# One fp32 product per block in place of three fp16 products in an attention kernel

## What is computed

```
att = softmax(einsum('bmi,bmj->bij', k, q), axis=2)          # layer 0, per image
out = x + einsum('cm,bmn->bcn', wo, einsum('bij,bmj->bmi', att, v))
...
scores = where(causal, -1e30, einsum('bhqd,bhkd->bhqk', q, k) / D ** 0.5)   # layer 1
attn = softmax(scores, axis=-1)
out = einsum('bhqk,bhkd->bhqd', attn, v) ... @ Wo
```

## Time and profile before

| what | value |
|---|---|
| median of 3 runs | 653.6 us |
| the profiled execution's own time | 655.42 us |
| its span | 653.6 us |
| granted TensorE clock, mean share of full speed | 0.94 |
| busy: PE, DVE, ACT, POOL | 535.2, 497.6, 468.7, 442.0 us |

### The profile page before, as it was taken

How to read it: one execution, slowest core, us unless ns; L and a number is a source line. 1 busy time by engine, 2 the same in 40 slices (tenths; PEclk the granted TensorE clock), 3 DMA queues, 4 the chain that set the end, 5 groups by cost and what they waited for, 6 DMA issues and landing times.

```text
span 653.6 us, 17645 instructions
## 1 busy us (share of the span) xinstructions
PE 535.2 (82%) x6985; PEld 348.9 (53%) x6985; DVE 497.6 (76%) x1060; ACT 468.7 (72%) x891; POOL 442.0 (68%) x401
## 2 busy tenths in 40 slices
PE   3777769799779999878989977878999988984694
PEld 0234347466546666546666644555666655663241
DVE  4667877688888778888778888886777888845568
ACT  2167648998748888757888865567888867892673
POOL 2455647978848878757878874476888767893003
PEclk9978769999979999989999998799999989996798
DMA  8000000000000000000000000000000000000001
GB/s 225 33 2 2 1 1 3 2 2 2 3 2 2 2 3 2 2 1 3 2 2 3 2 2 2 3 1 1 2 3 2 2 2 3 3 3 2 0 0 64
DMA packets 2784, 6.46 MB, mean 10 GB/s; under 512 B 1008, under 2 KB 1296, under 8 KB 2576
## 3 DMA queue, kind: packets, MB, share of 16 engines
q1 hardware_dynamic: 2336, 4.30, 2.4%
q10 hardware_dynamic: 368, 1.05, 0.5%
HBM read 4.22 MB, written 1.05 MB: 8 GB/s over the span
## 4 chain that ended last, share of the span: by engine, by line
PE 48%; DVE 31%; ACT 8%; POOL 6%; issue 5%; DMA 1%; DVEq 0%; SPq 0%; ACTq 0%; POOLq 0%
PE bank L355 7%; DVE attn_partial_max L667 7%; POOL probs_low L637 5%; PE bank L381 5%; PE bank L382 5%; PE bank L318 4%; PE bank L408 4%; DVE queries_low L660 4%; PE bank L412 4%; PE bank L410 4%; ACT queries_high L540 4%; PE bank L319 3%; PE bank L514 3%; DVE probs_low L637 2%; DVE conv_partial_max L656 2%
## 5 line engine op out<-in xcount | busy, mean ns | idle before, releaser
L637 POOL TENSOR_TENSOR probs_low<-probs,probs_high 128x512 f16<-128x512 f32 x312 | 374.7, 1223 | 135.2 <-ACT probs_high L553 134.9
L552 ACT ACTIVATE probs<-bank 128x512 f32<-128x512 f32 x352 | 219.3, 623 | 26.3 <-PE bank L384 19.3
L553 ACT ACTIVATE probs_high<-bank 128x512 f16<-128x512 f32 x352 | 220.6, 627 | 0.0
L667 DVE TENSOR_REDUCE attn_partial_max<-bank 128x1 f32<-128x512 f32 (+2 forms) x288 | 195.1, 686 | 24.8 <-PE bank L355 16.9
L408 PE MATMUL bank<-values_high,probs_high 128*128 128x65 f16 x1408 | 169.8, 198 | 6.0 <-POOL probs_low L637 2.5
L410 PE MATMUL bank<-values_low,probs_high 128*128 128x64 f16 x1408 | 169.8, 196 | 0.0
L412 PE MATMUL bank<-values_high,probs_low 128*128 128x65 f16 x1408 | 169.5, 196 | 0.0
L408 PEld LDWEIGHTS bank<-values_high,probs_high 128*128 128x128 f16 x1408 | 135.8, 100 | 31.2 <-issue 7.3
L410 PEld LDWEIGHTS bank<-values_low,probs_high 128*128 128x128 f16 x1408 | 133.9, 101 | 21.6 <-issue 4.2
L355 PE MATMUL bank<-attn_keys,queries_high 128*128 128x512 f16 (+3 forms) x384 | 117.1, 332 | 34.2 <-DVE attn_partial_max L667 22.2
L412 PEld LDWEIGHTS bank<-values_high,probs_low 128*128 128x128 f16 x1408 | 134.0, 100 | 0.0
(11 more groups left out here) (152 smaller groups left out, 737.3 us busy)
## 6 DMA issues: line engine op xcount, KB each, us to landing
x_channels<-in_x_cm SPq DMA_DIRECT2D x7, 256.0 KB, 9.0
tokens<-in_x_tm SPq DMA_DIRECT2D x1, 1024.0 KB, 12.0
out<-ln_channels SPq DMA_DIRECT2D x4, 256.0 KB, 2.0
queries_high<-minus_max_rows SPq DMA_DIRECT2D x36, 2.0 KB
attn_weights<-in_attn_w ACTq DMA_DIRECT2D x1, 512.0 KB, 8.6
x_channels<-in_x_cm ACTq DMA_DIRECT2D x1, 256.0 KB, 3.7
constants<-in_const ACTq DMA_DIRECT2D x1, 256.0 KB, 5.9
conv_weights<-in_conv_w SPq DMA_DIRECT2D x1, 128.0 KB, 2.4
```

Source lines behind the costliest of these rows:

```text
L552: nc.scalar.activation(e32[:, i % E_RING, :], o[:], ACT.Exp, scale=scale)
L553: nc.scalar.activation(p_hi[:, i % P_RING, :], o[:], ACT.Exp, scale=scale).then_inc(s_probs, 1)
L637: eng.tensor_tensor(out=p_lo[:, i % P_RING, :], in0=e32[:, i % E_RING, :], in1=p_hi[:, i % P_RING, :], op=ALU.subtract).then_inc(done, 1)
L667: nc.vector.reduce_max(dst, src, AX).then_inc(s_prep_used, 1)
```

## The change

Probabilities stay in fp32 in one ring of ten buffers, written by one exponential per item. Values stay in fp32, written by one ACT copy. Each block takes one fp32 product in place of three of fp16. The subtractions for `probs_low` and `values_low` are gone from POOL and DVE, with their semaphores, and LAG goes from 5 to 3.

```diff
-ST_RING, MX_RING, P_RING, E_RING, Q_RING = 3, 2, 8, 6, 3
-LAG, REST_LAG = 5, 3
-CONV_DVE_RESTS, ATTN_DVE_RESTS = (5, 11), (4,)
+ST_RING, MX_RING, E_RING, Q_RING = 3, 2, 10, 3
+LAG = 3
...
             nc.tensor.wait_ge(s_probs, i + 1)
-            if rest_on_dve(i):
-                nc.tensor.wait_ge(s_rest_dve, dve_rests(i))
-            else:
-                nc.tensor.wait_ge(s_rest_pool, i + 1 - dve_rests(i))
-            hi, lo = p_hi[:, i % P_RING, :], p_lo[:, i % P_RING, :]
-            vh, vl = v_hi[v % 2], v_lo[v % 2]
+            probs, values = e32[:, i % E_RING, :], v32[v % 2]
...
-                    nc.tensor.matmul(dst, hi[:, cols], vh[:, j, :], start=opens, stop=False,
-                                     skip_group_check=True)
-                    nc.tensor.matmul(dst[:, 0:C], hi[:, cols], vl[:, j, :], start=False, stop=False,
-                                     skip_group_check=True)
-                    ins = nc.tensor.matmul(dst, lo[:, cols], vh[:, j, :], start=False, stop=True,
-                                           skip_group_check=True)
+                    ins = nc.tensor.matmul(OT[c][:, t * PO:t * PO + PO], probs[:, cols], values[:, j, :],
+                                           start=opens, stop=True, skip_group_check=True)
...
             if i >= E_RING:
-                if rest_on_dve(i - E_RING):
-                    nc.scalar.wait_ge(s_rest_dve, dve_rests(i - E_RING))
-                else:
-                    nc.scalar.wait_ge(s_rest_pool, i - E_RING + 1 - dve_rests(i - E_RING))
-            if i >= P_RING:
-                nc.scalar.wait_ge(s_values, i - P_RING + 1)
+                nc.scalar.wait_ge(s_values, i - E_RING + 1)
-            nc.scalar.activation(e32[:, i % E_RING, :], o[:], ACT.Exp, scale=scale)
-            nc.scalar.activation(p_hi[:, i % P_RING, :], o[:], ACT.Exp, scale=scale).then_inc(s_probs, 1)
+            nc.scalar.activation(e32[:, i % E_RING, :], o[:], ACT.Exp, scale=scale).then_inc(s_probs, 1)
...
-                nc.scalar.activation(v_hi[k % 2][:, :, 0:C], AUX[:].rearrange("p (t c) -> p t c", c=C),
-                                     ACT.Copy).then_inc(s_aux_cast, 1)
+                nc.scalar.activation(v32[k % 2][:, :, 0:C], AUX[:].rearrange("p (t c) -> p t c", c=C),
+                                     ACT.Copy).then_inc(s_aux_used, 1)
...
-        def rest_item(eng, i, done):
-            eng.wait_ge(s_probs, i + 1)
-            eng.tensor_tensor(out=p_lo[:, i % P_RING, :], in0=e32[:, i % E_RING, :], in1=p_hi[:, i % P_RING, :],
-                              op=ALU.subtract).then_inc(done, 1)
...
-            elif what == "values":
-                nc.vector.wait_ge(s_aux_cast, AUX_CASTS_BY[m])
-                nc.vector.tensor_tensor(out=v_lo[k % 2][:], in0=AUX[:].rearrange("p (t c) -> p t c", c=C),
-                                        in1=v_hi[k % 2][:, :, 0:C], op=ALU.subtract).then_inc(s_aux_used, 1)
```

More of the change, by code:

```diff
@@ L122, in auxes_at @@
     return [m for m, step in enumerate(AUXES) if step[0] == g]
[L125 to L132, removed]
 def build(nc, x_cm, x_tm, conv_w, conv_vo, attn_w, ffn, gb, const, out):
@@ L177, in build @@
         q_lo = [sb(f"queries_low{i}", [P, N], f16) for i in range(Q_RING)]
[L178 to L182, removed]
+        e32 = sb("probs", [P, E_RING, CW])
+        v32 = [sb(f"values{i}", [P, NT, PO]) for i in range(2)]
         scaled = sb("scaled_outputs", [P, NC, TPC, C])
@@ L257, in build @@
         s_probs = sem("probs_written")
-        s_rest_pool = sem("rest_by_pool")
-        s_rest_dve = sem("rest_by_dve")
         s_values = sem("values_accumulated")
@@ L406, in pe_values @@
                     cols = slice((at + k) * P, (at + k + 1) * P)
-                    dst = OT[c][:, t * PO:t * PO + PO]
-                    nc.tensor.matmul(dst, hi[:, cols], vh[:, j, :], start=opens, stop=False,
-                                     skip_group_check=True)
-                    nc.tensor.matmul(dst[:, 0:C], hi[:, cols], vl[:, j, :], start=False, stop=False,
-                                     skip_group_check=True)
-                    ins = nc.tensor.matmul(dst, lo[:, cols], vh[:, j, :], start=False, stop=True,
-                                           skip_group_check=True)
+                    ins = nc.tensor.matmul(OT[c][:, t * PO:t * PO + PO], probs[:, cols], values[:, j, :],
+                                           start=opens, stop=True, skip_group_check=True)
             ins.then_inc(s_values, 1)
@@ L824, in _ @@
                 nc.vector.memset(amx[i][:], -3e38)
-                nc.vector.memset(v_hi[i][:, :, C:PO], 1.0)
+                nc.vector.memset(v32[i][:, :, C:PO], 1.0)
                 nc.vector.memset(y16[i][:, :, 0:1], 0.0)
@@ L835, in _ @@
                         dve_rowmax(v)
-                if 0 <= g - REST_LAG < ITEMS and rest_on_dve(g - REST_LAG):
-                    rest_item(nc.vector, g - REST_LAG, s_rest_dve)
                 for m in auxes_at(g):
@@ L965, in _ @@
             for g in range(0, LAST_SLOT):
-                if g < ITEMS and not rest_on_dve(g):
-                    rest_item(nc.gpsimd, g, s_rest_pool)
                 for v, c in HALVES_AT.get(g, ()):
@@ L1014 @@
 CASTS_BY = [sum(k < (4 if v < B else 2) for _, v, k in PREPS[:m + 1]) for m in range(len(PREPS))]
-AUX_CASTS_BY = [sum(what in ("conv_matrix", "values", "matrix") for _, _, what, _ in AUXES[:m + 1])
+AUX_CASTS_BY = [sum(what in ("conv_matrix", "matrix") for _, _, what, _ in AUXES[:m + 1])
                 for m in range(len(AUXES))]
```

## The result

The changed kernel takes **735.4 us** (median of 4 runs, 730.0 to 736.0) against 653.1 us (median of 4): 1.125 times as long, 95% interval 1.119 to 1.131. The prediction was 723 us, with 700 to 770 as its range. Medians and ratios in this document leave out two executions in a slow state: one of the kernel before, 682.0 us at a granted clock of 0.83, and one of the kernel with all three pieces put back, 1295.6 us, whose cause is not known.

What follows compares the result with a forecast made beforehand. The prediction took PE to set the pace of quiet causal units. Conv -1, causal +70 and end 0 gave +69 us on the 653.6 us median, so 723 us, with 700 to 770 as the range.

Steps and rivals of the forecast that it cites:

- What bounds the kernel: Causal units: PE sets the pace, busy 11.78 of 12.55 us, with ACT and POOL close behind.
- Price of the products: Item's products on PE: load-bound fp32 passes of 0.112 us, 0.84 us an item, 0.47 us more than in fp16.
- True fp32 in four passes: Products on PE: a skill rule of four passes, at fp16 pace 0.50 us an item, some 630 us in all.
- A quiet unit: Causal unit without layer norms: 12.55 + 4.2 - 0.45 = 16.3 us, bounds 16.0 to 17.2.
- The last interval: End of the causal stretch, taken to hold no preparation: 12.8 us, from 10.0.
- The extras: Causal time beyond quiet units, where layer norms are spread: 12 us left of 57, bounds 4 and 25.
- The conv stretch: Four conv units, 105.7 us before: PE's added work fits into its waits, -1 us, between -7 and +6.
- The end: Last items and recurrent layer: PE instead of POOL sets the last items' pace, 18.4 us against 18.2; 0 us change.
- rival 1: Fp32 products on PE: loads hide, streaming bounds a pass at 0.055 us; 613 us, faster; chance 0.07.
- Rival 2: PE between fp16 and fp32 products: changing type costs 0.25 us, up to 88 us on 352 items; about 800; chance 0.08.
- Rival 3: Runs of fp32 loads: clock falls to 1.2 GHz, a third of units twice as long; over 850 us; chance 0.05.
- Rival 4: Layer-norm units: extras do not shrink as PE's waits on DVE's queue stay; 745 to 769 us; chance 0.17.

Runs made afterwards that it cites:

- all three pieces put back: The relieved kernel with POOL's subtractions, ACT's second exponential and DVE's subtractions and low part of the values restored; 642.8 us, ratio 0.985 to the kernel before.
- the relieved kernel: The changed kernel with probabilities and values in fp16 and three fp16 products per block, all of high parts; 591.7 us, ratio 0.906 to the kernel before.
- the probe: The changed kernel with fp32 and fp16 test products added behind its last step; sixteen fp32 passes took 1.70 us with 8 moving columns, 1.78 with 128.
- the product alone: The kernel before with one fp32 product per block, both exponentials, the subtractions and LAG 5 kept; 769.0 us, ratio 1.180 to the kernel before.

## Why the prediction was right, and where it was off

The time came out inside the range, 12 us above the forecast, and the mechanism was right in the main. That it is only 12 us is in part luck, since errors of opposite sign met.

**What bounds the kernel**: right. PE set the pace of a quiet unit before, and does after; ACT and POOL, at 10.9 and 10.8 us of 12.55, were not its bound, as the relieved kernel with the same unit shows.

**Price of the products**: the pass of 0.112 us was right, to the digit, and its reason too, the load. Wrong was the end of the run. The step said that a run takes "7 x 0.112 + 0.055", with the stream of 65 columns behind the last pass. It takes 0.11 us there, as the probe shows for 8 to 128 columns. The rows of L462, with 512 columns, hide this, since their stream of 0.43 us is longer. By itself this term is 352 x 0.055 = 19 us. But the start of the run was wrong the other way: behind a 512-column product the first two passes are 0.056 us apart, not 0.112, so such a run takes the forecast 0.84 us by luck. The mean of 0.874 us in the causal stretch is 0.034 above the forecast, 0.3 us a unit and 10 us on its 288 items.

**True fp32 in four passes**, which the prediction set against its price: the trace has two instructions a product, 2816 for 1408. Set against fp16 products, one costs seven times as much at 65 columns (0.22 to 0.031 us) and four times at 512 (0.86 to 0.217 us).

**A quiet unit**: 16.57 us for 16.3, which is the 9 x 0.034 = 0.3 us of its runs. The wait for DVE went, the wait for ACT stayed, both as forecast.

**The last interval**: 14.4 us for 12.8. I had said that it holds no preparation, but nine products of L339, for maxima, are in it, where a full unit has twelve.

**The extras**: 7 us for 12, inside the bounds of 4 and 25. Both reasons hold: the longer slot covers the norms (57 to 25 us with the product alone), and the relief shortens DVE's chains (25 to 7 us; how much of this is POOL's was run apart only with fp16 products, 18 to 38 us).

**The conv stretch**: +4.3 us for -1, inside -7 to +6. The prediction reckoned at full clock, and at full clock it was near: in the probe's execution, the same kernel up to its last step, the clock stayed at 1.00 and this stretch took 106.3 us, +0.6. The other 3.7 us go with the 6.8 us at half clock.

```profile
26.48:132.82 106.34, 96.57 (x749) 77.55 (x750) 63.70 (x134) 49.46 (x87) 5.07 (x7) 1.00 0.01 1
```

**The end**: +0.8 for 0.

**The sum**, by the profiled spans: +80.5 us, where I had +69: conv 5 us more, causal 5 more, end 1 more. In the causal part 8 us of the units and 2 of the last interval stand against 5 that the extras fell short; without that the miss would be 17 us. One sign was off: ACT was to be near 250 us busy and is at 308.9. The rows of the exponentials overlapped (0.62 us each, 0.48 apart), so that the loss of one took 160 us off ACT's busy time, not its own 219.

**The rivals.** The loads don't hide (rival 1), as the probe shows for 8 to 128 columns; and a kernel whose products do cost as little as fp16 ones is faster than before, as that rival said, at 592 us with three of them. Rival 2 was wrong as told (no 0.25 us per change of type; before a run there is no gap) but right in kind: behind a run the next product comes 0.055 us later than reckoned. The 0.20 us behind L450 came back in the probe behind the run with 64 rows and in none with 128. Rival 3 did not happen in the causal stretch, where the clock is granted 1.00; in the conv stretch the clock fell for 6.8 us, behind waits of PE, and not in the probe's execution. Rival 4 did not happen either.

## What to carry to other kernels

Price an fp32 product by its loads: two passes, 0.11 us each for a stationary operand of 128 columns, however few columns move (8 to 128 here, at the upper clock), where an fp16 product with a load costs 0.03 us. Three fp16 products of 65 columns (0.09 us) are cheaper than one of fp32 (0.22 us); with 512 columns, where the stream sets both, the probe's fp16 products stand (745.46 - 744.81) / 3 = 0.217 us apart and L462's passes 0.43, so it would be 0.65 against 0.86, still not in favour of fp32, but no longer 2.4 times. Before crediting relief on other engines, look at a unit in which nothing special happens: if it does not get shorter, the relief is worth only what the special units lose. That can still be much: here 61.6 us with fp16 products, so that the relief was worth having and the fp32 product was not.

## What was not expected of the hardware

An fp16 product behind an fp32 pass starts 0.11 us behind it, whether 8 columns stream or 128. Its load is shown with 0.18 us behind 8 columns, 0.15 behind 65 and 0.10 behind 128, so the length of the load is not what sets the 0.11, and what does was not found. An fp32 pass behind an fp16 product of 65 columns has no such cost (0.03 us). The load of an fp32 operand with 64 columns makes a pass of 0.06 us.
